# An audio-tower kernel: the expert mask turned on VectorE in one 32-column block, and TensorE's pairs from the fifth on one projection unit later

## What is computed

```python
h = gelu(x[:, 1:] @ W[:D] + x[:, :1] @ W[D:] + b)          # 374 tokens of 256
y = layernorm(h)
h = h + softmax(cosine(y, y)) @ y + y                       # attention by cosine
z = layernorm(h)
logits = normalised(z) @ normalised(sim) - sigmoid(gates)   # 8 experts
mask = logits > 0, or the best 2 experts where none is      # 374 x 8, of 0 and 1
q, k, v = (sum over e of mask[:, e] * (z @ proj[e]) for proj in (q_proj, k_proj, v_proj))
o = softmax(causal(q @ k.T)) @ v
h = h + sum over e of (mask * softmax(logits over mask))[:, e] * (o @ o_proj[e])
```

## Time and profile before

| | |
|---|---|
| median of 3 runs | 711.66 us (711.36 to 711.82) |
| the profiled execution's own time | 711.77 us |
| its span, first to last instruction | 710.1 us |
| TensorE busy | 705.5 us, 99% |
| VectorE busy | 579.8 us, 82% |
| GpSimd busy | 400.5 us, 56% |
| ScalarE busy | 378.9 us, 53% |
| TensorE's granted clock over the span | 1.0 (2.4 GHz) |

### The profile page before, as it was taken

One profiled execution on the slowest core, in us unless ns is written; L12 is line 12 of the kernel. 1 busy time (PEld: TensorE's weight loads), 2 busy tenths in 40 slices (PEclk: granted clock), 3 DMA queues, 4 the chain that ended last, 5 costly groups with the idle time before them and its releaser, 6 DMA issues.

```text
span 710.1 us, 18197 instructions
## 1 busy us (share of the span) xinstructions
PE 705.5 (99%) x5440; PEld 473.1 (67%) x5440; DVE 579.8 (82%) x1455; ACT 378.9 (53%) x808; POOL 400.5 (56%) x655
## 2 busy tenths in 40 slices
PE   9999999999999999999999999999999999999998
PEld 8888666675757666575756666575766657575655
DVE  5788798888879888887979888887988888886736
ACT  4977373554646364563646355464646456364443
POOL 7652325756465566746566575746566674653434
PEclk9999999999999999999999999999999999999999
DMA  9581220202020120202020020202011020201111
GB/s 246 150 188 46 74 45 8 72 3 63 14 63 14 13 65 0 71 7 63 14 55 22 9 68 0 70 8 63 14 23 55 0 71 7 63 17 46 22 68 37
DMA packets 33558, 34.35 MB, mean 48 GB/s; under 512 B 7304, under 2 KB 29304, under 8 KB 33400
## 3 DMA queue, kind: packets, MB, share of 16 engines
q1 hardware_dynamic: 33136, 33.65, 18.4%
q10 hardware_dynamic: 392, 0.32, 0.1%
HBM read 27.70 MB, written 6.26 MB: 48 GB/s over the span
## 4 chain that ended last, share of the span: by engine, by line
PE 98%; issue 1%; POOL 0%; POOLq 0%; DVE 0%; ACT 0%; DVEq 0%
PE bank L1671 76%; PE bank L1734 7%; PE bank L1588 5%; PE bank L1645 3%; PE bank L1577 2%; PE bank L1805 2%; PE bank L1720 1%; PE bank L1783 1%; PE bank L1593 1%; PE bank L1612 1%; PE bank L1756 0%; PE bank L1745 0%; PE bank L1748 0%; POOL region_c L670 0%; POOL region_c L663 0%
## 5 line engine op out<-in xcount | busy, mean ns | idle before, releaser
L1671 PE MATMUL bank<-xm,w_qkv 128*128 128x374 f16 x2304 | 415.7, 322 | 0.0
L1671 PEld LDWEIGHTS bank<-xm,w_qkv 128*128 128x128 f16 x2304 | 220.8, 98 | 139.2
L908 ACT ACTIVATE region_c<-bank,out_w 128x256 f32<-128x256 f32 x180 | 84.8, 471 | 163.2 <-PE bank L1671 162.2
L1274 DVE TENSOR_TENSOR xm<-xT,mask_all 128x1496 f16<-128x1496 f16 x128 | 151.9, 1209 | 0.0
L1671 PE MATMUL bank<-w_o,aoT 128*128 128x512 f16 x540 | 143.3, 379 | 0.0
L1180 DVE SCALAR_TENSOR_TENSOR h<-bank,out_w,h 128x256 f32 (+1 forms) x180 | 86.5, 481 | 48.8 <-ACT region_c L908 43.9
L663 POOL TENSOR_TENSOR region_c<-region_c 128x512 f32<-128x512 f32 x46 | 77.1, 1675 | 27.8 <-ACT region_c L908 22.8
L692 POOL TENSOR_TENSOR exp_hl<-exp,exp_hl 128x128 f16<-128x128 f32 (+2 forms) x48 | 41.9, 875 | 83.7 <-ACT exp_hl L864 83.2
L1671 PEld LDWEIGHTS bank<-w_o,aoT 128*128 128x128 f16 x540 | 50.4, 98 | 39.5
L1159 DVE TENSOR_SCALAR region_b<-h,moments,small 128x256 f32 (+1 forms) x96 | 48.8, 553 | 6.1 <-POOL small L577 6.1
L670 POOL TENSOR_TENSOR region_c<-region_c 128x256 f32<-128x256 f32 x46 | 46.9, 1019 | 8.1 <-POOL region_c L663 7.9
(11 more groups left out here) (200 smaller groups left out, 1067.6 us busy)
## 6 DMA issues: line engine op xcount, KB each, us to landing
mask_all<-d_mask SPq DMA_DIRECT2D x32, 384.0 KB, 3.9
h<-in_x_dram SPq DMA_DIRECT2D x16, 256.0 KB, 5.0
out_dram<-h SPq DMA_DIRECT2D x31, 128.0 KB
rnorm_row<-d_rnorm SPq DMA_DIRECT2D x16, 192.0 KB, 4.1
h<-in_x_dram SPq DMA_DIRECT2D x15, 112.0 KB, 5.4
out_dram<-h SPq DMA_DIRECT2D x15, 112.0 KB
xm<-in_L_ffn_q_proj_dram SPq DMA_DIRECT2D x2, 512.0 KB, 7.5
region_c<-in_L_ffn_k_proj_dram SPq DMA_DIRECT2D x2, 512.0 KB, 6.4
```

The source lines that it names most:

```text
L908: a.activation(prod[:, prod_buf(n, t), q, :], pair_bank(n, p)[:, C:2 * C], ACT.Copy, scale=weights_out(n)[:, t, 2 * q + 1:2 * q + 2]).then ...
L1274: v.tensor_tensor(xm[:, e, :, 0:T], xT[1][:, :, :, 0:T].rearrange("p a c t -> p (a c) t"), mask_all[:, e, 0:T].unsqueeze(1).broadcast_to([ ...
L1671: last = t_.matmul(dst, left[lp], right[rp], start=(starts and k == 0), stop=(stops and k == 2), skip_group_check=True)
```

## The change

The three transposes on TensorE and the copy on ScalarE go. `route` writes the mask of all three tiles side by side into one tile of 128 tokens by 32 columns (24 used). VectorE turns it in one instruction (`turn_mask`, after the add of pair 2) as four blocks of 32 by 32, so that block q has the 24 rows of tokens 32 q to 32 q + 31. SyncE stores each block with a DMA of its own, in such an order in DRAM that the loads stay as they were. The waits that kept PSUM banks and the old tiles apart go. The dummy matmuls and the first activation at the start read another zeroed tile. On TensorE the pairs 4 to 10 come behind the next projection unit than before, and pair 11 comes behind the transposes of `turn_first` instead of ahead of them.

```diff
@@ buffers
-        mask16 = sb("mask16", [P, NT, P], F16)
-        maskT = sb("maskT", [E, TP], F16)
+        mask16 = sb("mask16", [P, SQ], F16)
+        mask_turned = sb("mask_turned", [P, SQ], F16)
@@ SyncE, mask_around(f)
-                sp.dma_start(d_mask[f, :].rearrange("(e t) -> e t", e=E), maskT[:, :]).then_inc(s_mask_stored, 16)
-                sp.wait_ge(s_mask_stored, 16 * (f + 1)).then_inc(s_sp_passed, 1)
+                rows = d_mask[f, :].rearrange("(r b j) -> b r j", r=SQ, j=SQ)
+                for q in range(P // SQ):
+                    sp.dma_start(rows[q][0:NT * E, :], mask_turned[q * SQ:q * SQ + NT * E, :]).then_inc(s_mask_stored, 16)
+                sp.wait_ge(s_mask_stored, 16 * (P // SQ) * (f + 1)).then_inc(s_sp_passed, 1)
@@ ScalarE
-            def turned_mask(f):
-                act.wait_ge(s_mask_turned, f + 1)
-                if later(f):
-                    act.wait_ge(s_mask_stored, 16 * f)
-                a.activation(maskT[:, :], as16(turn[1] if later(f) else turn[0], TP)[0:E, :], ACT.Copy).then_inc(s_mask_row, 1)
@@ VectorE, route(b)
-                if later(b):
-                    dve.wait_ge(s_mask_turned, b)
-                v.tensor_tensor(mask16[:, :, 0:E], lg[:, 0, :, :], M, ALU.add).then_inc(s_mask_ready, 1)
+                v.tensor_tensor(mask16[:, 0:NT * E].rearrange("p (e t) -> p t e", t=NT), lg[:, 0, :, :], M,
+                                ALU.add).then_inc(s_mask_ready, 1)
@@ VectorE
+            def turn_mask(b):
+
+                dve.wait_ge(s_mask_ready, 2 * b + 1)
+                if later(b):
+                    dve.wait_ge(s_mask_stored, 16 * (P // SQ) * b)
+                v.transpose(mask_turned[:, :], mask16[:, :]).then_inc(s_mask_row, 1)
@@ VectorE, a full step
                     route(f)
-                    pairs(2, 4)
+                    pairs(2, 3)
+                    turn_mask(f)
+                    pairs(3, 4)
                     weight_max(f)
@@ TensorE
-            def turn_mask(f):
-                pe.wait_ge(s_mask_ready, 2 * (f + 1))
-                pe.wait_ge(s_T2_lo, f + 1)
-                for t in range(NT):
-                    last = t_.transpose(as16(turn[1] if later(f) else turn[0], TP)[:, t * P:(t + 1) * P], mask16[:, t, :], ident16[:, :])
-                last.then_inc(s_mask_turned, 1)
@@ TensorE, a full step
                     pair(n, 3)
-                    M(15)
-                    turn_mask(f)
+                    M(15, 16)
                     pair(n, 4)
-                    for k in range(7):
-                        M(16 + k)
+                    for k in range(6):
+                        M(17 + k)
                         pair(n, 5 + k)
                     if g1 is not None:
                         turn_first(g1)
+                    pair(n, PAIRS - 1)
                     M(23)
```

More of the change, by code:

```diff
@@ L35, in audio_tower_kernel @@
     PAIRS = NT * E // 2
+    SQ = 32
     KEYS = [min((i + 1) * P, T) for i in range(NT)]
@@ L101, in audio_tower_kernel @@
         row3 = sb("row3", [P, 6, NT])
-        mask16 = sb("mask16", [P, NT, P], F16)
-        maskT = sb("maskT", [E, TP], F16)
+        mask16 = sb("mask16", [P, SQ], F16)
+        mask_turned = sb("mask_turned", [P, SQ], F16)
         mask_all = sb("mask_all", [P, E, TP], F16)
+        zeros16 = mask_all[:, 0, 0:P]
         route_w = sb("route_w", [P, B, NT, E])
@@ L160, in audio_tower_kernel @@
         d_route = nc.dram_tensor("d_route", [(NT - 1) * E * P], F32, kind="Internal").ap()
-        d_mask = nc.dram_tensor("d_mask", [B, E * TP], F16, kind="Internal").ap()
+        d_mask = nc.dram_tensor("d_mask", [B, SQ * P], F16, kind="Internal").ap()
         bank = [ctx.enter_context(nc.psum_tensor(f"bank{i}", [P, 512], F32)) for i in range(8)]
@@ L751, in _ @@
             act.wait_ge(s_pad_zeroed, 1)
-            a.activation(unused[:, :], mask16[:, 0, 0:1], ACT.Gelu)
+            a.activation(unused[:, :], zeros16[:, 0:1], ACT.Gelu)
             def split_in(b):
@@ L1040, in _ @@
             exp_cosines(1, (2,))
-            turned_mask(0)
             route_exp(0)
@@ L1054, in _ @@
             v = nc.vector
-            v.memset(mask16[:, 0, :], 0.0).then_inc(s_pad_zeroed, 1)
+            v.memset(zeros16, 0.0).then_inc(s_pad_zeroed, 1)
             v.memset(h[96:P, 0:1, NT - 1, :], 0.0).then_inc(s_zeroed, 1)
@@ L1064, in _ @@
             v.memset(read_hl[:, :], 0.0).then_inc(s_zeroed, 1)
-            v.memset(mask16[:, 1:NT, :], 0.0)
+            v.memset(mask16[:, :], 0.0)
             def token_weights_low():
@@ L1543, in _ @@
             route(0)
+            turn_mask(0)
             weights_low(2)
@@ L1611, in _ @@
             for k in range(WARM):
-                t_.matmul(bank[6][:, 0:P], mask16[:, 0, :], mask16[:, 0, :], start=True, stop=True)
+                t_.matmul(bank[6][:, 0:P], zeros16, zeros16, start=True, stop=True)
             pe.wait_ge(s_consts, 1)
@@ L2023, in _ @@
             turn_in(13)
-            turn_mask(0)
             dots(1, 2)
```

7 lines of the change are left out of this document (removed).

## The result

The change made the kernel **slower: 720.90 us** (median of 4 runs, 720.62 to 721.22) against 711.51 for the kernel before (4 runs, 711.27 to 711.82), a ratio of 1.0131 [1.0116, 1.0146]. The forecast was 719.7 in a range from 714.5 to 722.8.

The account below looks back on a forecast made before the run. TensorE was taken as the bound, with VectorE's train from pair 8 arriving just in time. 13 x 0.61 = 7.9, +0.6 for step 16, -0.3 for early mask turnings: +8.2, giving 719.9, stated as 719.7 us, range 714.5 to 722.8.

Parts of the forecast that it names:

- a train on VectorE that starts with pair 8 arrives just in time: From pair 8 to the turning of exponentials, VectorE works almost unbroken; its low part has 0.07 us to spare.
- Removed, -2.7: Three mask transposes on TensorE in each of 16 steps, 56 ns each, were to give back 2.7 us.
- Added, 0: One VectorE transpose behind pair 2's add and four DMA issues in place of one were to be hidden, costing 0.
- Moved, +0.61 a period: Pair 8 one unit later: a 0.78 us stall at the turning of exponentials, less 0.17 saved, in 13 periods.
- Part of that stall already shows earlier ... 0.2 to 0.3 us: At the first cosine product TensorE waits 0.2 to 0.3 us for ScalarE's second copy, not added to the stall.
- GpSimd's adds of a tile are themselves moved with the pairs, so I let the pattern stand: In VectorE's six mask products, turns with GpSimd were to stay as before, with only 0.1 us off the first product.
- pairs 4 to 7 start a train on VectorE with idle time of 0.9 to 1.0 us ahead of each add: Moved pairs 4 to 7 were to have room on VectorE, as ahead of pair 8's add.
- Tail and head: Step 15 into 16 was to cost +0.6 us once; two mask turnings before the first full step to save 0.3.
- the first stretches of the loop may have a little more room: Reason given at the loop's start for saying 719.7 us instead of 719.9.
- no product waits for the mask's DMA: Rival, chance 0.06: the four small stores bring the mask late, the first product waits; one microsecond more gives 733.
- no moved pair waits for an add: Rival, chance 0.05: moved pairs upset something earlier, such as pair 11 waiting for pair 9's add; 721 to 724.
- ScalarE's copies are a second bound: Rival, chance 0.10: VectorE catches up, the wait at the first cosine product stays; 712.5 to 714.5 us.

Follow-up runs that it names:

- e3: The kernel after the change, with pair 11 again ahead of the twelve transposes and pairs 4 to 10 still one unit later: 721.00 us.
- e6: The kernel after the change, with pair 11 ahead of the transposes and, in the loop, the fifth mask product on 64 of 374 columns: 710.36 us.
- e7: The kernel after the change, with the pairs from the fifth on two units later than before instead of one: 733.59 us.
- e2: The kernel before, with its mask still turned on TensorE, and only the pairs moved as in the change: 723.01 us.
- e1: The kernel after the change, with TensorE's pairs at their old places, so only the mask's new way is left: 711.07 us.
- e5: e4 with the wait for the turned rows' low part asked last of three ahead of the first cosine product: 715.52 us.
- e4: The kernel after the change, with pairs 4 to 7 at their old places and only pairs 8 to 11 one unit late: 717.15 us.
- e8: The mask's new way with pair 4 alone one unit later and all else at its place of before: 719.94 us.
- e9: e8 with VectorE's routing sum and ScalarE's routing exponential ahead of pair 4's add and scaling: 709.37 us.
- e10: The kernel after the change, with routing sum and exponential ahead of pair 4's add and scaling: 714.95 us.

## Why the prediction was right

**Direction, size, place and releasers hold.** 8.2 us were forecast and 9.4 measured in the medians (9.0 in the spans of the profiled executions). By its steps:

*"a train on VectorE that starts with pair 8 arrives just in time"*: right. The train ended 14.07 behind the pair before and 14.00 after; the add starts 1.55 behind its pair in both. e3 takes the hole at ScalarE's copies away and the loss stays; e6, from there, cuts the train and the loss goes. e7 (a unit more, 0.95 a period more) shows that it is no loss of fixed size.

*Removed, -2.7*: the size per transpose is right (e2 against the kernel after: 0.17 a period), but what the prediction didn't see is that in the old order it was not there to be had. By e1 the mask alone brings 0.8 us. The add of pair 2 and the wait of pair 4 for it, 0.125, lay under the transposes. "Three transposes in each of 16 steps" was costed by what they take; the step asked what the transposes cost and not what they cover. The term was saved by the moved pairs, which cover pair 4 in their turn.

*Added, 0*: right. 0.20 us were taken for the transpose and 0.20 measured. The four issues took 1.82 us and not 1.2, and the loads started 3.60 behind the transpose's end where 2.9 to 3.2 were reckoned; the room for that was there, so the stores delayed nothing.

*Moved, +0.61 a period*: the mis-sized term. It was to be a stall of 0.78 less 0.17; measured are 0.41 + 0.39 + 0.06 = 0.86 less 0.17, so +0.69. Of the 0.08 missing, 0.06 are the hesitations behind the hole. 0.1 was taken off the train, and 0.07 came off it (14.07 to 14.00). The 13 periods came to +8.73 (0.44 for the first, 8.30 for the others) where 7.9 was forecast.

*"Part of that stall already shows earlier ... 0.2 to 0.3 us"*: too small. The 2.72 from pair 11 to the end of the second copy were right to the hundredth; the hand-over is 0.24 and not 0.06. About half of it is the wait that stood behind the late one: with the late one last, 0.12 are left (e5: 585.83 against 584.90 + 0.81). In the step written out behind the loop, with the order of before, the load starts 0.07 behind the copy (631.36 against 630.48 + 0.81), so the long hand-over is seen only in the loop. Why, no run separates further. 0.24 + 2.72 - 2.55 is the 0.41 of the trace. As the prediction said, it was not to be added: e3 takes it away and the time stays.

*"GpSimd's adds of a tile are themselves moved with the pairs, so I let the pattern stand"*: right for this change, and it was the assumption with the most hanging on it. It holds because both ends moved by one unit: pair 4, behind which the routing weights stand, and pair 8. With only pair 8 moved (e4) the train is 13.44, with only pair 4 (e8) 14.95. The prediction named the pairs themselves as the reason; e8, e9 and e10 show that it is the routing weights behind pair 4. In e10 the same pairs are moved, GpSimd does not follow, and 5.9 of the 9.4 us are gone: that the forecast's number held here was in part luck. The table of waits (total us, times, longest) has it in the kernel after:

```profile
POOL lg L650 <- DVE row L1345: 33.8, 16, 6.3
```

Before, the same wait (L647 there) was 24.1 us over its 16 times. It is idle time of an engine that is busy for 56%, and it is what kept GpSimd's place beside pair 8.

*"pairs 4 to 7 start a train on VectorE with idle time of 0.9 to 1.0 us ahead of each add"*: a wrong reading. The earlier trace rows show it for pair 8 only; in the same timeline there is 0.88 us ahead of pair 7's add, and under 0.2 ahead of those of pairs 4, 5 and 6. In the kernel after it cost nothing, but pair 4 alone moved ends 8.2 us above the kernel before (e8), by way of GpSimd.

*Tail and head*: +0.6 was forecast for step 16 and -0.3 for two early mask turnings. From the last turning to the end it is +0.26, in which step 16's new waits (0.165 ahead of the scores' third product and 0.278 ahead of the turning of probabilities, 0.44 together) stand against the 0.17 of the transposes saved in step 15. Of the two early turnings one saved its 0.17; beside the other two waits grew, by 0.14 and 0.16, so the first turning behind a full step comes at the same time. Head and tail together were forecast at +0.3 and came to +0.25: both terms were too large, and that they cancel is luck. And the first of the 13 periods cost 0.44 only ("the first stretches of the loop may have a little more room").

None of the rivals occurred in the kernel after: no product waits for the mask's DMA, the turning still waits for the train when the hole at ScalarE's copies is over, and no moved pair waits for an add. That ScalarE's copies are a second bound close under the train's was right all the same (e4, e5, e10).

## What to carry to other kernels

An engine that is busy all the time need not be the only bound: look for the chain on another engine that ends within a tenth of a microsecond of where it is waited for, and find what starts it; work moved from behind that start to ahead of it is paid for in full. Before an instruction is taken off the busy engine, ask which wait it covers. Where two engines slow each other, moving the start of one of them changes how long both take, so move both ends together or free both, as e9 does.

## What the runs showed of the hardware

*VectorE's products and GpSimd's work take turns.* A mask product that is issued while a GpSimd instruction runs ends 0.79 us behind that instruction's end (586.22 + 1.46 = 587.68 against 584.93 + 1.96 = 586.89 in the kernel after; 585.26 against 584.47 in e8; 624.25 against 623.45, 0.80, in e4). The GpSimd instruction that is queued behind it ends 1.13 us (128x512) or 0.59 us (128x256) behind the product's end (586.89 against 585.76, 588.27 against 587.68). The adds of the pairs take no part in it: the one at 585.82 in the kernel after lasts its usual 0.48 us in the middle of GpSimd's L666. The Trainium skill ("SBUF — State Buffer", Terms) says that the two engines share a port pair which one of them holds for its whole instruction while the other waits; the products' rows agree, and they show what the page doesn't tell, that the same instructions make a train of 13.44 to 14.95 us by how they meet.

*Where the wait stands among waits.* In the hardware loop, with a further wait behind the late one, the weight load started 0.24 us after the copy that released it; with the late one last 0.12 (e5); in the step written out behind the loop, with the further wait, 0.07; and behind the turning's single wait 0.05. Putting the late one last gave 0.1 us a period back (40.89 to 40.78), 1.3 us over the 13 periods.

*Three transposes on TensorE cost 0.17 us in a period* (e2 against after), though one lasts 0.22 us. The Trainium skill ("TensorE: Matmul & The Clock Gate", Part 4) has about 0.275 us for one within a kernel; by that figure, an estimate, 48 of them would have been 13 us, and the best kernel here gained 2.1.
